# Ranks behind the next preparation, mixed output between down products, second skip term a group later, other low parts on VectorE, half block shared

## The reference

```
x = x + xattn(layernorm(x), k, skip, ctx, ctx)     # 32 filters k of 512 taps, 8 rows share one
    kv[i, j] = v[i] * c[j]                           # all 64 pairs of the 8 rows of one filter
    y = causal_convolution(kv, k) + kv * skip[i]
    out[j] = sum_i y[i, j] * c[i]
x = x + ffn(layernorm(x))
    shared: silu(x @ wg.T) * (x @ wu.T) @ wd.T       # hidden size 704
    routed: the 2 best of 8 experts (hidden size 352), weights from sigmoid(x @ gate_w.T), scaled to sum 2.5
```

## Time and profile before

| what | value |
|---|---|
| runs | 769.8 us median of 3 (769.48 to 770.99) |
| profiled execution | 771.41 us, its span 769.6 us |
| PE | 679.9 us busy, 88% of the span, mean granted clock 0.96 |
| VectorE, GpSimd, ScalarE | 434.9, 387.1, 288.2 us busy |
| `products` of four banks, `total` | 2.47 and 2.29 us |
| skip product; skip term | 0.75 alone, up to 2.33; 0.69 and 0.69 |
| skip sum; half of a `prepare` | 0.86 from start to start; 0.87 |
| statistics of four tiles | 2.47 us |
| `pick`; `pairs` | 149.99 to 151.9; 168.25 to 172.7 us |
| row sends on POOL | eight, 196.12 to 206.4 us |

### The profile page before, as it was taken

How to read it: one execution, slowest core, us unless ns; L and a number is a source line. 1 busy time by engine, 2 the same in 40 slices (tenths; PEclk the granted TensorE clock), 3 DMA queues, 4 the chain that set the end, 5 groups by cost and what they waited for, 6 DMA issues and landing times.

```text
span 769.6 us, 11432 instructions
## 1 busy us (share of the span) xinstructions
PE 679.9 (88%) x3552; PEld 343.8 (45%) x3553; DVE 434.9 (57%) x662; ACT 288.2 (37%) x362; POOL 387.1 (50%) x333
## 2 busy tenths in 40 slices
PE   1786977969989969989999988798999999999992
PEld 1333433424444434444444433334566666665661
DVE  4798689667975666877695685872311111111110
ACT  4436646444223534223531257452322222222220
POOL 2889988385782574783867107700222322222231
PEclk9998998989999989999999999989899999999998
DMA  7933223601334600314224288986765565656533
GB/s 206 270 89 95 88 78 68 151 6 23 131 76 100 147 14 29 123 29 81 58 68 156 78 252 291 316 174 171 113 94 93 85 89 90 94 82 93 91 50 41
DMA packets 101364, 84.28 MB, mean 110 GB/s; under 512 B 68064, under 2 KB 81888, under 8 KB 100768
## 3 DMA queue, kind: packets, MB, share of 16 engines
q1 hardware_dynamic: 92128, 65.16, 33.5%
q0 software_dynamic: 9200, 18.65, 13.7%
HBM read 44.35 MB, written 25.68 MB: 91 GB/s over the span
## 4 chain that ended last, share of the span: by engine, by line
PE 59%; DVE 14%; ACT 9%; POOL 8%; issue 5%; DMA 3%; SPq 1%; POOLq 0%; another core or an unknown queue 0%; DVEq 0%; ACTq 0%
PE banks L734 18%; PE banks L736 18%; PE banks L735 18%; POOL arena L584 5%; POOL arena L609 2%; DVE stats L1243 2%; DVE arena L1230 2%; DVE mixT L1237 2%; PE banks L756 2%; PE banks L930 2%; ACT arena L1068 2%; DVE arena L1216 1%; DMA arena<-split_filters 1%; DVE hm L1364 1%; DMA stages<-in_expert_w 1%
## 5 line engine op out<-in xcount | busy, mean ns | idle before, releaser
L584 POOL TENSOR_TENSOR arena<-arena 128x512 f32<-128x512 f32 x124 | 136.1, 1129 | 67.0 <-DVE arena L1216 65.7
L697 POOL DMA_INDIRECT out<-xf,ids x39 | 60.8, 1559 | 198.8 <-ACT xf L1154 95.6
L734 PE MATMUL banks<-arena 128*128 128x512 f16 x320 | 125.3, 392 | 19.6 <-DVE arena L1230 9.7
L735 PE MATMUL banks<-arena 128*128 128x512 f16 x320 | 125.3, 392 | 0.6 <-issue 0.6
L736 PE MATMUL banks<-arena 128*128 128x512 f16 x320 | 125.1, 391 | 0.0
L1230 DVE TENSOR_TENSOR arena<-banks,arena 128x512 f32<-128x512 f32 x128 | 81.5, 683 | 38.3 <-PE banks L736 37.9
L734 PE MATMUL banks<-arena,normed 128*128 x312 | 98.4, 315 | 0.4 <-issue 0.4
L735 PE MATMUL banks<-arena,normed 128*128 x312 | 98.3, 315 | 0.0
L736 PE MATMUL banks<-arena,normed 128*128 x312 | 98.2, 315 | 0.0
L989 ACT ACTIVATE arena<-arena 128x2048 f16<-128x2048 f32 x31 | 59.1, 1907 | 87.3 <-POOL arena L584 87.2
L609 POOL TENSOR_TENSOR arena<-arena 128x512 f16<-128x512 f32 x68 | 78.8, 1191 | 7.6 <-ACT arena L989 7.5
(11 more groups left out here) (164 smaller groups left out, 1132.3 us busy)
## 6 DMA issues: line engine op xcount, KB each, us to landing
arena<-split_filters SPq DMA_DIRECT2D x32, 256.0 KB
arena<-in_expert_w SPq DMA_DIRECT2D x12, 544.0 KB, 8.2
stages<-in_expert_w SPq DMA_DIRECT2D x10, 544.0 KB, 6.2
arena<-in_ctx_hidden SPq DMA_DIRECT2D x4, 1024.0 KB, 8.1
arena<-in_ctx SPq DMA_DIRECT2D x8, 512.0 KB, 6.5
x_tok<-in_x SPq DMA_DIRECT2D x6, 512.0 KB, 7.4
out<-x_tok SPq DMA_DIRECT2D x6, 512.0 KB, 5.4
x_tok<-in_expert_w SPq DMA_DIRECT2D x5, 544.0 KB
```

Source lines behind the costliest of these rows:

```text
L584: nc.gpsimd.tensor_tensor(kv[s % 2][:, lb * COLS:(lb + 1) * COLS].rearrange("p (b j i) -> p b j i", i=NH, j=NH), v[:, a, None, :].to_broad ...
L697: nc.gpsimd.indirect_dma_start(out=out, out_offset=bass.IndirectOffsetOnAxis(ap=ids[slot][:, 0:1], axis=0), in_=yg[slot], in_offset=None, ...
L734: nc.tensor.matmul(dst, wh, xh, start=(k == 0), stop=False)
L735: nc.tensor.matmul(dst, wh, xl, start=False, stop=False)
```

## The change

Six edits, all but the last of them in the order of work.

1. `DVE_LOWS`: of the steps 0 to 13 DVE makes low parts 0, 1, 3, 5, 7, 9, 11 instead of 0, 1, 5, 8, 10, 12; from step 14 on both have the even ones.
2. The skip term of group 1 is computed in group 1, behind `gate_up(0, 0)` and `gate_up(0, 1)`, not in group 0 beside convolutions 5 and 6. The load of context 2 moves to the end of group 1 with it.
3. `prepare(g + 1)` comes later (behind `gate_up(g - 1, 2)` and convolution h = 5), and `ranks` and `pairs` come behind it; the turn banks' order follows.
4. `mix_out` is in halves with `down(g - 2, 0)` between; `mixed` takes the statistics of the first two tiles before the last two are added.
5. In group 1 products 9 stand ahead of `feed_low`, piece 6 of the shared weights comes a step later; in group 2 and 3 `add_shared(g - 2, 0)` is ahead of `total`.
6. Block 0 of the hidden layer: its low part is written to rows 64 to 127 of `hTh` block 0, and the matching rows of `d_h` hold the same weights again (loaded twice from memory), so one matmul of 128 rows replaces two of 64. `down_products` issues 17 matmuls for `down`'s 18.

```diff
-DVE_LOWS = (0, 1, 5) + tuple(range(HG, H, 2))
+DVE_LOWS = (0, 1, 3, 5, 7, 9, 11) + tuple(range(2 * HG - 2, H, 2))
...
-        turn_order = [("prep", 0), ("skip", 0), ("prep", 1), ("skip", 1)]
+        turn_order = [("prep", 0), ("skip", 0), ("prep", 1)]
         for g in range(1, G):
-            turn_order += [("out", g - 1), ("feed", g - 1), ("xf", g - 1), ("rank", g - 1)]
-            turn_order += [("prep", g + 1), ("skip", g + 1)] if g < G - 1 else []
+            turn_order += [("out", g - 1), ("feed", g - 1), ("xf", g - 1)]
+            turn_order += [("skip", 1)] if g == 1 else []
+            turn_order += [("prep", g + 1)] if g < G - 1 else []
+            turn_order += [("rank", g - 1)]
+            turn_order += [("skip", g + 1)] if g < G - 1 else []
...
             def load_shared(i):
+                if i == DOWN_AT:
+                    sp.dma_start(shared_raw(i)[:, L:SH_PIECE], shared_w[:, L:SH_PIECE]).then_inc(shared_in[i], 16)
+                    for copy in range(2):
+                        sp.dma_start(shared_raw(i)[copy * HALF:(copy + 1) * HALF, 0:L], shared_w[0:HALF, 0:L]
+                                     ).then_inc(shared_in[i], 16)
+                    return
...
-                if g < G - 1:
+                if 1 < g < G - 1:
                     load_context(g + 1)
...
+                    if g == 1 and h == HG - 1:
+                        load_context(2)
...
+            def down_products(g, q, first=0, end=SM):
+
+                dst, c = down_bank(g, q), slice(q * P, (q + 1) * P)
+                for k in range(first, end):
+                    w = slice(k * L, (k + 1) * L)
+                    nc.tensor.matmul(dst, hTh[:, k, c], d_h[:, w], start=(k == 0), stop=False)
+                    if half_tile(k):
+                        last = nc.tensor.matmul(dst, hTh[0:HALF, k, c], d_l[0:HALF, w], start=False, stop=False)
+                    else:
+                        nc.tensor.matmul(dst, hTl[:, k, c], d_h[:, w], start=False, stop=False)
+                        last = nc.tensor.matmul(dst, hTh[:, k, c], d_l[:, w], start=False, stop=(k == SM - 1))
+                return last
...
             prepare(1)
-            convolve(5)
-            skip_sum(1, 0)
-            skip_sum(1, 1)
-            convolve(6)
-            skip_sum(1, 2)
-            skip_sum(1, 3)
-            convolve(7)
+            for s in range(5, HG):
+                convolve(s)
             for g in range(1, G):
                 s0 = g * HG
                 convolve(s0)
-                mix_out(g - 1)
+                mix_out(g - 1, range(0, 2))
                 if g > 1:
                     if g == 2:
                         pe.wait_ge(shared_l, SH_PIECES)
-                    for q in range(Q):
+                    down(g - 2, 0)
+                mix_out(g - 1, range(2, Q))
+                if g > 1:
+                    for q in range(1, Q):
                         down(g - 2, q)
...
                 convolve(s0 + 3, range(LB - 1, LB) if g == 1 else range(LB))
+                if g == 1:
+                    skip_sum(1, 0)
+                    skip_sum(1, 1)
                 gate_up(g - 1, 1)
-                ranks(g - 1)
                 convolve(s0 + 4)
+                if g == 1:
+                    skip_sum(1, 2)
+                    skip_sum(1, 3)
+                gate_up(g - 1, 2)
                 if g < G - 1:
                     prepare(g + 1, range(0, 2))
-                gate_up(g - 1, 2)
+                convolve(s0 + 5)
                 if g < G - 1:
                     prepare(g + 1, range(2, Q))
-                for h in range(5, HG):
+                gate_up(g - 1, 3)
+                ranks(g - 1)
+                for h in range(6, HG):
                     convolve(s0 + h)
...
-                nc.vector.tensor_tensor(hTl[p, bass.ds(m, 1), :].rearrange(one), hm[p, :],
-                                        hTh[p, bass.ds(m, 1), :].rearrange(one), ALU.subtract).then_inc(hl_ready, 1)
+                low = hTh[HALF:2 * HALF, 0:1, :] if half_tile(m) else hTl[p, bass.ds(m, 1), :]
+                nc.vector.tensor_tensor(low.rearrange(one), hm[p, :], hTh[p, bass.ds(m, 1), :].rearrange(one), ALU.subtract
+                                        ).then_inc(hl_ready, 1)
...
             def mixed(g):
 
                 for q in range(Q):
-                    if g == G - 1 and q == 2:
-                        expert(0, 1)
+                    if q == 2:
+                        if g == G - 1:
+                            expert(0, 1)
+                        dve.wait_ge(x1_done, Q * g + q)
+                        tile_moments(x_tok[g % 3], range(0, 2))
...
                 pick(g - 1)
+                if g == 1:
+                    skip_product(1, 0)
+                    skip_product(1, 1)
                 for h in range(3, HG):
                     if h > 3:
                         low_parts(s0 + h + 1)
-                    if h == 4:
+                    if h == 6:
                         pairs(g - 1)
...
+                    if g == 1 and h in (3, 4):
+                        skip_term(1, 2 * h - 6)
+                        skip_term(1, 2 * h - 5)
```

62 lines of the change are left out of this document (30 added, 32 removed).

## The result

The changed kernel takes 777.3 us (median of 4 runs, 774.6 to 778.5), the one before 769.6. The ratio is 1.0095, 95% interval 1.0064 to 1.0126: 0.9% slower. The forecast was 744 us. The profiled execution took 774.55 us, its span 772.8.

What follows compares the result with a forecast made beforehand. TensorE, 88% busy, was taken as the bound except from 50 to 115 us, where GpSimd was. Leads of 23.4 through group 3's opening, 1.1 and 1.6 summed to 26.1 us off 769.8: forecast 744, range 730 to 759.

Steps and rivals of the forecast that it cites:

- The end of the groups: Later pairs delay low parts, POOL's outer products and eight row sends, not PE; lead 23.4 us after group 3 opens.
- Groups 2 and 3: Down product between mix_out's halves covers 2.24 us; with clock and down savings 5.9, lead 20.0 at convolution 17.
- Rest of group 1 and of group 2: Later ranks remove waits of 2.20 and 5.15 us in group 1; leads 14.1 at convolution 16, 18.5 after group 2.
- Group 0: Redistributed low parts and the postponed skip term bring PE to mix_out(0) 14.2 us earlier, 3.4 of it only put off.
- rival C: Shared SBUF port: low parts and skip products cost DVE 1.0 and POOL 1.9 us more each; 749 to 758, chance 0.20.
- Head of PE's queue: Group 1, skip sums ahead of gate_up(0, 1): 5.8 us new wait for DVE's skip product; lead 7.5 at convolution 12.
- rival D: Skip sums heading PE's queue hold all of group 1, skip product at 164 instead of 138; some 775, chance 0.03.
- Hidden layer: At gate_up(1, 2): PE waits 4.0 us for DVE's hm, plus 2.0 of slow clock.
- Half block: In each down product: 17 full matmuls with no change of rows save 0.33 to 0.4 us; the sum takes 0.4.
- End: After the groups: split moments gain 1.1 us and the last four down products 1.6; routed tiles untouched.
- Rival E: Expert weights' transfers after 437 us set the end, 10 to 26 us given back; 754 to 770, chance 0.04.
- B: Rival: new waits stay hidden at filter 12, SP's queue and convolution 11; 731 us, chance 0.20.

Runs made afterwards that it cites:

- f1: Changed kernel, unchanged, run again beside the kernel before: 776.1 us, ratio 1.0093.
- f2: Changed kernel with the last root moved ahead of the eight pair sends of group 2: 767.5 us, ratio 0.9976 to the kernel before.
- g2: Kernel before with only the pair sends of group 2 moved behind the last root: 768.3 us, ratio 0.9989.
- g1: Changed kernel with group 2 pair sends behind the last root, add_shared(g-2, 1) ahead of mixed_shift, low part s0+2 behind it: 755.7 us, ratio 0.9827 to before.
- c2: Changed kernel without the down product between mix_out's halves or split moments, add_shared(g-2, 0) back behind mixed_shift: 765.2 us, ratio 1.0013 to before.
- a3: Changed kernel with add_shared(g-2, 1) ahead of mixed_shift and the feed's low parts: 764.6 us, ratio 1.0015 to the kernel before.
- f3: Changed kernel with second skip term, ranks and pairs back; add_shared(g-2, 1) and low part s0+2 earlier, group 2 pair sends later: 753.1 us, ratio 0.9789 to before.
- d4: Changed kernel with ranks and pairs ahead of the next preparation again in all groups: 761.7 us, ratio 0.9880 to the kernel before.
- d2: Kernel before with only the new low-part split, the root behind the low part and the seventh piece a step later: 765.0 us, ratio 0.9922.
- c1: Kernel before with only the half block shared, 17 matmuls per down product instead of 18: 764.8 us, ratio 1.0001.
- f4: Changed kernel with ranks and pairs early again in group 3 alone: 767.4 us, ratio 0.9975 to the kernel before.
- d3: Changed kernel with the second skip term back in group 0: 774.4 us, ratio 1.0046 to the kernel before.

## Why the prediction was wrong

The sign and most of the size come from the end of the groups and from the down products; most waits that the forecast named came much as it said. The shortfall at the marks (lead forecast less lead measured) is 5.5 us at `mix_out(0)`, 3.3 at convolution 12, 6.8 at 16, 14.3 at 17, 12.5 at 24, 19.8 at 25, 26.0 at `mix_out(3)` and 29.3 at the last matmul: 14.8 come at the down products of groups 2 and 3 and 6.2 between convolution 25 and `mix_out(3)`.

**The end of the groups (failed, 6.2 us at the marks, 8.6 in the times of f1 and f2, of the 33 us between 744 and 777).** The step is the sentence "`pairs` (4.4 on DVE) now delays products 14, low part 16 and so POOL's outer 18 and the eight row sends behind it, not PE." I carried the delay of the sends forward in group 1 and priced it at nothing, and in group 3, where sixteen sends follow one another, not at all. f2 puts a number on it: 776.1 to 767.5 us for the place of eight issues, and g2 shows that the kernel before doesn't pay it for those eight. The rows to see it by were there, in the trace of the kernel before, VectorE and GpSimd in time:

```profile
427.41 0.69 DVE L1230 TENSOR_TENSOR arena<-banks,arena 128x512 f32<-128x512 f32 x1 [7.81 <-PE banks L736]
```
```profile
425.51 0.96 POOL L633 DMA_INDIRECT pair_table<-pair,row  x1 [0.30 <-issue]
```

The fourth product of convolution 30 waits 7.81 us and starts behind the last send. It costs PE next to nothing there, and the working did not ask where it would go when `pairs` moved. Nor did it ask why the halves of `mix_out` were 2.24 us apart: most of that is a late increment too, so the 2.24 and 2.28 us that the sum takes back there hang on the sends too.

**Groups 2 and 3 (failed, by 7.5 and 7.3 us at the marks of convolutions 17 and 25).** The step is "A down product between the halves of `mix_out` covers the 2.24; with the clock behind it (2.0) and the down products' saving, 5.9". The wait is gone, but the step left out what the down products wait for. Each from the third on takes a bank that `add_shared` of two before must have read; the second of these sums stands behind two low parts of the feed, and these behind ScalarE. The fourth waits 4.55 us and the slow clock follows: 8.60 us from the third's start to the fourth's, where the second took 4.20. Forecast was a gain of 5.9 at convolution 17, measured a loss of 1.6, the same again at convolution 25 (+4.2 forecast, -3.1 measured). The lead of 11.9 in g1 at convolution 17, for 5.7, shows the size of it, and c2 that it isn't the interleaving but the lead itself that runs into the unmoved sums. The 2.8 us of wait forecast before `gate_up(1, 1)` came as 0.27, since TensorE was late itself; in a3, where it wasn't, it is 3.44.

**Rest of group 1 and of group 2 (partly failed, some 2.5 us each).** The long waits for the ranks went as forecast: the lead rises to 10.9 at convolution 13. From there to 16 it falls to 7.3, and from 21 to 24 from 9.7 to 6.0. About 1.1 us of each fall is work put off behind that mark, which the forecast of group 2 had; 1.9 are three waits (0.30, 0.58, 1.03), where the late `pairs` meets the next group's skip products and sums (the 0.58 by `next_row` above is one; "none by `next_row`" was wrong). In f3, with early ranks, the lead stays at 8.0 and 10.8, in d4 at 2.4 and 5.3. So late ranks gain at convolution 16, as forecast, but d4 shows the gain lost again at the down products and the last sends: 1.2% below before, for the changed kernel's 0.9% above it. g1 against f3 says less once the repairs are made, 0.9827 and 0.9789, and no run parts the ranks' share of that from the skip term's.

**Group 0 (mis-sized, 5.5 us at `mix_out(0)`).** Low part 3 and the freed low parts did move PE up, 8.7 us for 14.2. Single traces scatter here by several us, so the size is uncertain. POOL isn't relieved: it works 64.67 of the 65 us. GpSimd and VectorE in time, after:

```profile
49.92 2.98 POOL L625 TENSOR_TENSOR rstd<-var_eps,con 128x4 f32<-128x4 f32 x1 [2.56 <-DVE var_eps L1282]
...
96.21 6.55 POOL L620 TENSOR_TENSOR arena<-arena 128x512 f16<-128x512 f32 x4
```
```profile
98.41 3.33 DVE L1249 TENSOR_TENSOR arena<-arena 128x2048 f16<-128x2048 f32 x1
```

The root took 2.98 us beside VectorE's low part 3, where the later ones take 1.0; low part 8 took 6.55 for 4.5 and started at 96.21 for 91.8. This is rival C at work in group 0, at about the price per instruction that C had (1.9 on POOL, 1.0 on DVE). It doesn't decide: d2, which has these very low parts without the rest of the change, is 0.8% faster than before. The trace agrees with the Trainium skill's rule (GPSIMD Engine Reference, section Key points) that GpSimd shares its SBUF interfaces with VectorE, and that VectorE instructions with two SBUF inputs contend with it.

**Head of PE's queue (right).** 4.83 us of wait for the skip product, for 5.8; rival D is refuted. Its 775 lies near the measured 777 by chance. At convolution 11 the 3.4 us came (3.36) but from the filter that ScalarE turned late, not from low part 11. **Hidden layer (right):** 3.70 us for 4.0 at `gate_up(1, 2)`. **Half block (mis-sized):** 0.4 a product in the sum, 4.8 us for twelve; 0.22 measured. The working took "no change of rows", but one matmul of 64 rows is left, and it starts 0.31 us behind the one before it and the next 0.32 behind it, for 0.215 (220.08, 220.39, 220.71 us in the trace of after). In c1 what the first eight save is taken back by the waits for their banks.

**End (mis-sized).** 2.7 us forecast, a loss of 0.6 to 1.5 measured behind `mix_out(3)`; its cause stays open. Rival E is refuted: f3 comes to that mark 16.5 us early and ends 18.1 early, so what is gained before it isn't given back to the experts' transfers. B didn't happen.

No rival was slower by a mechanism that acted. The 0.95 for faster rested on leads carried forward without walking the down products' semaphores and the last group's sends; and no rival asked for a loss there.

## What to carry to other kernels

When work is moved to an earlier place, walk every wait of what follows it, bank by bank, to the queue in which its releaser stands; a lead is given back where one engine arrives early at another's unmoved order. Three small reorderings (eight sends, one sum, one low part) turned +0.9% into -1.7%. Look in the trace before for stalls that cost nothing and ask what they are tied to, since moving that can lay them on the critical path.

## What the runs showed of the hardware

- In four of the six sets of runs, increments by TensorE came late beside runs of small indirect DMAs issued by GpSimd (eight of 128 rows of 8 bytes, 1.26 us each): 4 to 10 us late at convolution 30 or 31, while TensorE itself went on issuing matmuls. They reached VectorE between 1 us before the start of the last send (f4) and 3.7 us behind it (d3), and ScalarE once 3.3 us late (429.03 us, before). Not every increment is held: in the trace of before that of the third bank of convolution 16 took 0.42 us amid the sends. Behind sends of whole rows delays of 1.1 us are seen (f2 and g1). In two sets, one of them on the same chip, none of this happened (0.42 us at convolutions 30 and 31, VectorE waiting 1.90 us for 9.2 to 9.9). What makes the difference between the sets, and by which path the sends hold the increment, stays open; that the pair sends are needed for the long delay is shown by f2, which only moves them.
- The kernel before is 5 to 8 us slower in the sets in which increments come late (769 to 772 us for 764), with the wait between the halves of `mix_out` at 2.24 for 0.51 us. That the late increments are the whole of it isn't shown.
- A GpSimd root of 128x4 elements took 2.98 us beside a VectorE low part and 1.01 to 1.10 in the seven other places.
